# Weighting gathered rows from their own denominator columns, without a second copy of the exponentials in PSUM

## The reference, cut to what matters

```python
e = (left + right + em_e) / 3.0
e = jnp.where(e > 0, e, NEG_SLOPE * e)
e_max = jax.ops.segment_max(e, dst, num_segments=N)
e_exp = jnp.exp(e - e_max[dst])
e_sum = jax.ops.segment_sum(e_exp, dst, num_segments=N)
a = e_exp / e_sum[dst]
msg = feat_src[src] * a[:, :, None]
rst = jax.ops.segment_sum(msg, dst, num_segments=N)
```

## Time and profile before

| what | value |
|---|---|
| runs | 3052.17, 3049.98, 3046.11 us; median 3049.98 us |
| profiled execution | 3053.74 us |
| span of its instructions | 3052.0 us, 48723 instructions |
| mean granted clock of TensorE | 0.943 of full speed |
| busy: PE, DVE, POOL, ACT | 2645.6 us (87%), 2223.2 us (73%), 2005.0 us (66%), 1652.6 us (54%) |
| HBM | 205 GB/s over the span |

### The profile page before, as it was taken

The page is one execution under the profiler, slowest core; times in us unless marked ns, Lnnn a source line. Parts: engine busy times, 40 slices in busy tenths (PEclk is TensorE's granted clock), DMA queues, the critical chain, the costliest instruction groups (busy, mean ns, idle before and its releaser), DMA issues.

```text
span 3052.0 us, 48723 instructions
## 1 busy us (share of the span) xinstructions
PE 2645.6 (87%) x13426; PEld 1861.6 (61%) x13426; DVE 2223.2 (73%) x7629; ACT 1652.6 (54%) x3538; POOL 2005.0 (66%) x2041
## 2 busy tenths in 40 slices
PE   7698888888888888979999998899999988988894
PEld 5466666666666666746666664566666655655562
DVE  6369899899898988845666665566666656878885
ACT  5347776777677666635554553455555533444430
POOL 3576666666666666357776665777766757777772
PEclk9689999999999999979999999999999998999996
DMA  8766777777777776567776763777766557777762
GB/s 236 214 189 197 211 216 215 216 211 211 217 217 212 216 199 199 158 209 217 222 222 207 216 196 118 238 227 222 216 206 191 176 179 227 244 238 240 240 207 71
DMA packets 455091, 630.35 MB, mean 207 GB/s; under 512 B 94496, under 2 KB 373088, under 8 KB 454816
## 3 DMA queue, kind: packets, MB, share of 16 engines
q0 software_dynamic: 97184, 280.55, 33.0%
q1 hardware_dynamic: 325568, 301.63, 31.7%
q10 hardware_dynamic: 32064, 44.98, 4.0%
HBM read 551.28 MB, written 75.63 MB: 205 GB/s over the span
## 4 chain that ended last, share of the span: by engine, by line
PE 50%; ACT 19%; issue 10%; DVE 9%; POOL 5%; DMA 2%; ACTq 0%; SPq 0%; DVEq 0%; POOLq 0%
PE ps L1297 21%; ACT one_hot L2187 7%; PE ps L1874 7%; PE ps L1349 5%; PE ps L1371 4%; ACT root L2221 4%; PE ps L1335 4%; POOL ring L1242 3%; PE ps L1921 3%; PE ps L1309 3%; ACT attention_work L2175 3%; PE ps L1882 2%; POOL ring L621 2%; DVE block_cube L798 1%; PE ps L692 1%
## 5 line engine op out<-in xcount | busy, mean ns | idle before, releaser
L1242 POOL DMA_INDIRECT ring<-message_table,src_index x1209 | 1183.1, 979 | 559.9 <-issue 379.4
L621 POOL DMA_INDIRECT ring<-attention_table,src_index x784 | 795.6, 1015 | 367.6 <-issue 211.0
L1297 PE MATMUL ps<-count_rows,high_rows 128*128 128x512 f32 x1764 | 759.5, 431 | 98.4 <-ACT attention_work L1629 71.5
L1297 PE MATMUL ps<-count_rows,low_rows 128*128 128x512 f32 x1764 | 719.9, 408 | 0.0
L1639 ACT ACTIVATE count_rows<-one_hot 128x512 fp32r<-128x512 uint8 x882 | 524.7, 624 | 185.7 <-PE ps L1297 174.1
L1297 PEld LDWEIGHTS ps<-count_rows,high_rows 128*128 128x128 f32 x1764 | 347.3, 197 | 214.2 <-issue 91.6
L2187 ACT ACTIVATE one_hot<-iota_row,dst_rel 128x128 f32<-128x128 f32 x784 | 241.2, 388 | 307.6 <-PE ps L1882 303.6
L1518 DVE CAST high_rows<-attention_work 128x512 fp32r<-128x512 f32 x441 | 192.7, 437 | 293.9 <-PE ps L1297 276.7
L1874 PE MATMUL ps<-ring,one_hot 128*128 128x265 f32 x1568 | 404.3, 402 | 1.8 <-issue 1.7
L1297 PEld LDWEIGHTS ps<-count_rows,low_rows 128*128 128x128 f32 x1764 | 347.3, 197 | 74.8
L1874 PEld LDWEIGHTS ps<-ring,one_hot 128*128 128x128 f32 x1568 | 308.6, 200 | 61.8 <-issue 5.1
(11 more groups left out here) (199 smaller groups left out, 3699.0 us busy)
## 6 DMA issues: line engine op xcount, KB each, us to landing
attention_work<-message_table SPq DMA_DIRECT2D x432, 256.0 KB
one_hot<-dense_adjacency SPq DMA_DIRECT2D x126, 448.0 KB, 4.2
attention_work<-in_dst_edges SPq DMA_DIRECT2D x112, 448.0 KB
ring<-message_table,src_index POOLq DMA_INDIRECT x1209
dense_adjacency<-root ACTq DMA_DIRECT2D x24, 784.0 KB, 4.4
attention_sums<-sums_out SPq DMA_DIRECT2D x112, 132.5 KB, 2.5
ring<-attention_table,src_index POOLq DMA_INDIRECT x784
message_table<-attention_work ACTq DMA_DIRECT2D x98, 128.0 KB, 3.2
```

The source lines that it names most:

```text
L621: pool.indirect_dma_start(m.ring[:, k, t, 0:cols], None, table, bass.IndirectOffsetOnAxis(ap=m.src[:, at:at + 1], axis=0)).then_inc(s[f"ro ...
L1242: pool.indirect_dma_start(m.quad_ring[:, k, j, :], None, m.tables[w.l], bass.IndirectOffsetOnAxis(ap=m.src[:, t:t + 1], axis=0)).then_inc( ...
L1297: last = nc.tensor.matmul(m.ps[:, 2 + half, 0:cols], rows[:, v % SPLITS, half * P:(half + 1) * P], m.a_rows[:, k, 0:cols], start=(j == 0 a ...
```

## The change

DVE's `weigh` waits for `denoms` and reads its weights from the denominator columns of the rows that it multiplies. The activation that wrote the exponentials to PSUM, its signal `expd`, its wait for `weighed` of two chunks ago and the PSUM buffers are gone. Nothing changes place.

```diff
 ATTENDED = dict(
-    scored=0, leaky=0, xt=1, bwd=0, mt=1, diff=1, expd=2, denoms=0, weighed=0, apart=0, onehot=0, shifted=0, summed=2, kept=2,
+    scored=0, leaky=0, xt=1, bwd=0, mt=1, diff=1, denoms=0, weighed=0, apart=0, onehot=0, shifted=0, summed=2, kept=2,
...
         def weigh(c):
 
             k = c % RING
-            dve.wait_ge(s["expd"].sem, s["expd"].done(c))
-            weights = m.weights[:, c % 2].rearrange("p (t h) -> p t h", h=HEADS)
+            dve.wait_ge(s["denoms"].sem, s["denoms"].done(c))
+            weights = ring_heads[k][:, :, :, HD]
             nc.vector.tensor_tensor(ring_heads[k][:, :, :, 0:HD], ring_heads[k][:, :, :, 0:HD],
                                     weights[:, :, :, None].to_broadcast([P, TILES, HEADS, HD]),
                                     ALU.mult).then_inc(s["weighed"].sem, 1)
...
             act.wait_ge(s["diff"].sem, s["diff"].done(c))
-            if c >= 2:
-                act.wait_ge(s["weighed"].sem, s["weighed"].done(c - 2))
-            nc.scalar.activation(m.weights[:, c % 2], m.diff, ACT.Exp, scale=1.0 / 3.0).then_inc(s["expd"].sem, 1)
             nc.scalar.activation(ring_heads[c % RING][:, :, :, HD], m.diff.rearrange("p (t h) -> p t h", h=HEADS), ACT.Exp,
                                  scale=1.0 / 3.0).then_inc(s["denoms"].sem, 1)
...
-        m.weights = m.ps[:, 2, 0:2 * 64].rearrange("p (k e) -> p k e", k=2)[:, :, 0:TILES * HEADS]
```

## The result

The changed kernel takes 3119.96 us (median of 5 runs, 3117.85 to 3125.39) against 3049.98 us: 1.0237 times the time of before, 95% interval 1.0225 to 1.025. It is slower by 70 us. The forecast was 3038.4 us, with 3047 us as the upper end, and "slower" had 0.06. The profiled execution has a span of 3116.1 us against 3052.0 us, so the 64 us to explain are in its trace.

A forecast was written before the change was run, and what follows sets the result against it. The prediction took a loop of waits between ACT and PE to bound the duo steps. Removing L2166 gave 83 x 0.14 = 11.6 us, all else nothing: 3049.98 - 11.6 = 3038.4 us, range 3030 to 3047 us.

The forecast's parts named there:

- What bounds the kernel: Attention stage, duo steps: a loop of waits between ACT and PE, containing L2166, sets the period of 10.56 us.
- the ACT term: Removing activation L2166 from the ACT-PE loop starts the pack 0.14 us earlier in 83 steps: 11.6 us gained.
- `weigh` released by L2167: On DVE, `weigh` waits for L2167 instead of L2166 and is released 0.09 us later; charged nothing, uncovered 3.5 us.
- its duration: `weigh` on DVE, reading its weights from SBUF, takes 0 to 0.05 us more per chunk; taken as 0.
- its slack: DVE's `below_max` is done 2.0 us before `soften` takes it, which covers the 0.09 us later release.
- The rivals: Prediction's step weighing three other outcomes: another path takes over (0.15), POOL and DVE contend in SBUF (0.05), more gained (0.06).
- the port: `weigh` with two SBUF inputs blocks POOL's gathers 2.0 us a chunk: 19 us lost, 3069 us; chance 0.05.
- The sum: Whole kernel: only the 11.6 us gain from removing L2166 counted, every other part at nothing, giving 3038.4 us.
- Other path: Duo steps: DVE or the path through the first cross takes over in some 60 steps, leaving 3 us gain, 3047 us; chance 0.15.
- full slot: Removing the activation frees its full 0.20 us plus 0.02 us handling in 96 steps: 21 us gained, 3029 us; chance 0.06.

The follow-up runs named there:

- the two six-gather kernels: The changed kernel and the kernel before, each without the seventh tile's gather from the eighth chunk on: 3038.65 and 3050.56 us, 0.9963 and 1.0006 of before.
- the first experiment: Kernel before, both activations kept, first copy of the exponentials moved from PSUM to its own SBUF buffer: 3108.04 us, 1.0206 of before; on a slow chip 0.9888.

## Why the prediction was wrong

**What bounds the kernel, and the ACT term: right.** The loop between ACT and PE set the period, L2166 stood in it, and one activation is worth 0.165 us a step over 95 steps, where the prediction had 0.14 us in 83. It came out as 15.7 us in the duo steps of the kernel with one activation and PSUM weights, and as 15.7 us between the two six-gather kernels, where 12 us were left of it in the time. In the changed kernel itself it shows for a dozen chunks.

**`weigh` released by L2167, its duration, its slack: right.** 1.992 us against 1.990; the prediction took 0 to 0.05 us. Charging nothing for the later release was right as well: two experiments gave DVE 0.4 us more a chunk or more still, for nothing. The 87 ns by which the activation into SBUF is longer are not all the price of SBUF over PSUM: into the plain SBUF buffer of the first experiment it took 234 ns, against 200 ns into PSUM and 286 ns into the strided denominator columns.

**The step that failed** is "The rivals", the port: 'Against it: L2105 and L2108, which have two SBUF inputs and also run beside gathers, hardly vary [...] and show neither a block nor being blocked.' The fact is true and says nothing: in this contest DVE isn't the one that waits. The row to ask was the gather's, and the way to ask it was by where a gather starts relative to such an instruction, not by a mean over all of them. The answer was in the trace of before: 150 gathers lengthened beside L1520 and L2108. The sum priced the second SBUF input on DVE alone, at 0 to 0.05 us, and put its cost on POOL at nothing; measured, L621's mean rose from 1.02 to 1.28 us in the stretch, which made POOL the bound. In the same step, "no row has an overlap as long as 2 us" hid that the law, end of the DVE instruction plus 0.82 us, could be read from overlaps of 0.4 and 0.7 us and carried over. With the hold, the rival's working gives a slowdown, not the forecast; so the chance of 0.05 was the error, and the range with it.

**The rival's size was off too,** 19 us against 70. It took 8.77 + 2.0 = 10.8 us a chunk; measured in the stretch it is 7 x (1.283 + 0.30) = 11.1 us by the mean of the gathers, and 10.98 us from one `weigh` to the next over the duo steps, against 10.55 us before. One reason is that the hold isn't `weigh` alone: a gather that starts in the 0.5 us of L1991 before it is held through both, as a rule up to 3.2 us, once 5.54 us. Another is the marks: without POOL's wait for PE more gathers start beside them, 166 with a mean of 1.37 us between 226 and 1240 us, against 146 with 1.22 us before. The largest is that it was counted over the 96 duo steps alone. 24 of the 64 us arose outside: 8 us before the ring was full, 16 us in the last 8 chunks, where the loop had been faster than POOL's new pace by far more than 0.2 us.

**Other path, full slot:** neither came about.

## What to carry to other kernels

Moving the second operand of a long DVE product from PSUM to SBUF can cost another engine: with two SBUF inputs it holds back gathers that POOL starts meanwhile, until it ends or longer. Before such an edit, add up POOL's busy time and the 0.30 us behind each gather, and compare the sum plus the hold with the period; if it fits, nothing happens once the ring is full, and if not, the ring's lead hides the loss for some chunks and then it is paid in full. To save the second activation, keep the operand in PSUM and let the product make the denominators (18 us faster here, 15 us of it in the stage). Where the operand must be in SBUF, cut the product and put other work between the pieces; with marks between them the loss was gone here, though some gathers were still held for 4 to 5 us.

## What was not expected of the hardware

- A gather that starts during one of these DVE instructions with two SBUF inputs ends 0.82 us after it in the median: L1520 of 0.69 us, L2108 of 0.42 us, L2014 of 1.99 us. One that starts before it, even by 0.02 us, or within the first 0.03 us of an L1520, is not held, unless another such instruction is running. DVE itself is hardly delayed, L2014 by 2 ns in the median and L1520 by at most 0.06 us.
- Seven such instructions without a gap hold like one (a gather of 2.09 us); with marks between them most gathers get in (1.49 us), while 15 of 683 took over 4 us.
- The marks, with one SBUF input in fp16, hold gathers too: 1.22 us in the mean of 146 in the kernel before, and 15 of them until 0.69 us after the last mark.
- The exact moment at which the port goes back between two overlapping DVE instructions is not settled.
- On another chip the kernel before took 3682 us in place of 3050, with POOL waiting for PE 345 us over the 112 chunks even beside the SBUF copy of the weights, and that copy cost nothing there. The hold by itself is not a loss; it becomes one where POOL is the bound.
